# A chain of four image layers on one Trainium2 core: the step input multiplied on VectorE, and the last two pairs of sixteen states summed by TensorE

## The reference, cut to what matters

```
delta = softplus(einsum('blr,dr->bld', dt, W_dt) + b_dt)
A = -exp(A_log)
def step(hst, xs):
    d_t, B_t, C_t, u_t = xs
    dA = exp(d_t[:, :, None] * A)
    hst = hst * dA + (d_t * u_t)[:, :, None] * B_t[:, None, :]
    y_t = einsum('bdn,bn->bd', hst, C_t)
    return hst, y_t
y = ys + xc * Dp
y = y * silu(z)
```

## Time and profile before

| | |
|---|---|
| time, median of 3 runs | 5245.92 us (5242.39 to 5246.16) |
| the profiled execution's own time | 5247.66 us |
| its span | 5245.8 us |
| TensorE (PE) busy | 4574.1 us, 87% |
| VectorE (DVE) busy | 4798.9 us, 91% |
| ScalarE (ACT) busy | 3722.0 us, 71% |
| GpSimd (POOL) busy | 4717.1 us, 90% |
| mean granted TensorE clock | 0.971 |

### The profile page before, as it was taken

The page is one execution under the profiler, slowest core; times in us unless marked ns, Lnnn a source line. Parts: engine busy times, 40 slices in busy tenths (PEclk is TensorE's granted clock), DMA queues, the critical chain, the costliest instruction groups (busy, mean ns, idle before and its releaser), DMA issues.

```text
span 5245.8 us, 62166 instructions
## 1 busy us (share of the span) xinstructions
PE 4574.1 (87%) x17331; PEld 2625.0 (50%) x17331; DVE 4798.9 (91%) x5978; ACT 3722.0 (71%) x6077; POOL 4717.1 (90%) x3342
## 2 busy tenths in 40 slices
PE   7469999999999999999999999999999999999880
PEld 7125555555555555555555555555555555555450
DVE  4689999999999999999999999999999999999933
ACT  3457777777777777777777777777777777777642
POOL 0599999999999999999999999999999999999910
PEclk9679999999999999999999999999999999999995
DMA  4466666666666666666666666666666666666618
GB/s 142 154 237 234 232 243 244 238 236 242 241 232 238 245 241 236 234 249 238 226 241 250 236 236 234 250 238 227 241 248 236 235 241 243 240 230 244 235 73 324
DMA packets 199100, 1216.88 MB, mean 232 GB/s; under 512 B 27880, under 2 KB 28656, under 8 KB 67696
## 3 DMA queue, kind: packets, MB, share of 16 engines
q1 hardware_dynamic: 194416, 1196.26, 62.1%
q10 hardware_dynamic: 4352, 16.78, 0.8%
HBM read 1158.43 MB, written 54.53 MB: 231 GB/s over the span
## 4 chain that ended last, share of the span: by engine, by line
PE 57%; issue 12%; ACT 12%; DVE 12%; POOL 3%; DMA 2%; SPq 0%; DVEq 0%; ACTq 0%; POOLq 0%
PE psT L880 29%; PE psE L880 15%; PE psT L1058 6%; PE psY L880 6%; DVE hs L567 5%; DVE nm L587 3%; ACT da L752 3%; ACT pt L760 2%; ACT p L794 2%; DVE psD L554 2%; POOL pa L370 2%; ACT L722 1%; ACT xc L722 1%; PE psD L880 1%; POOL pa L376 1%
## 5 line engine op out<-in xcount | busy, mean ns | idle before, releaser
L370 POOL TENSOR_TENSOR pa<-hs,rows_all 128x1024 f32<-128x1024 f32 x1024 | 2416.4, 2360 | 8.0 <-DVE hs L567 3.4
L752 ACT ACTIVATE da<-delta,neg_a 128x512 f32<-128x512 f32 x2048 | 1410.0, 715 | 103.7 <-DVE hs L567 85.9
L376 POOL TENSOR_TENSOR pa<-pa 128x512 f32<-128x512 f32 x1024 | 1310.0, 1279 | 40.1
L554 DVE TENSOR_TENSOR psD<-rows_all,psU 128x512 f32<-128x512 f32 x2048 | 1303.0, 681 | 4.8 <-DMA rows_all<-bc_scratch 3.8
L567 DVE TENSOR_TENSOR_SCAN hs<-da,hlast,psD 128x512 f32<-128x512 f32 x1024 | 1266.6, 1263 | 4.0 <-ACT da L752 3.9
L567 DVE TENSOR_TENSOR_SCAN hs<-da,psD 128x512 f32<-128x512 f32 x1024 | 1204.1, 1202 | 2.2 <-POOL hlast L374 1.5
L880 PE MATMUL psT<-pt,va 128*128 128x256 f32 x4096 | 964.2, 381 | 0.0
L760 ACT ACTIVATE pt<-psT 128x512 f32<-128x512 f32 x1024 | 606.3, 592 | 334.9 <-PE psT L1058 332.4
L880 PEld LDWEIGHTS psT<-pt,va 128*128 128x128 f32 x4096 | 746.7, 190 | 161.6 <-issue 76.9
L1058 PEld LDWEIGHTS psT<-ident,p 128*128 128x128 f32 x4096 | 483.7, 141 | 519.0 <-issue 359.7
L794 ACT ACTIVATE p<-psE,nm 128x1024 f32<-128x1024 f32 x512 | 570.1, 1113 | 234.6 <-DVE nm L587 232.6
(11 more groups left out here) (180 smaller groups left out, 4841.7 us busy)
## 6 DMA issues: line engine op xcount, KB each, us to landing
rows_all<-bc_scratch SPq DMA_DIRECT2D x1024, 1024.0 KB, 4.7
xin<-x SPq DMA_DIRECT2D x40, 512.0 KB, 7.7
xres<-x SPq DMA_DIRECT2D x64, 256.0 KB, 6.1
x_scratch<-x SPq DMA_DIRECT2D x32, 512.0 KB, 5.5
f_scratch<-fa SPq DMA_DIRECT2D x32, 512.0 KB, 6.8
xres<-x SPq DMA_DIRECT2D x8, 512.0 KB, 3.7
x1g<-x SPq DMA_DIRECT2D x8, 512.0 KB, 3.6
fa<-x SPq DMA_DIRECT2D x8, 512.0 KB, 3.7
```

What stands on the lines that cost most here:

```text
L370: pool.tensor_tensor(pa[:, k % PROD, :, :], hs[:, sl, :, :], rows_all[:, slot, 2:4, :], ALU.mult).then_inc(S["prod"], 1)
L376: pool.tensor_tensor(pa[:, k % PROD, 0, :], pa[:, k % PROD, 0, :], pa[:, k % PROD, 1, :], ALU.add).then_inc(S["pair"], 1)
L554: dve.tensor_tensor(psD[:, j, :], rows_all[:, slot, j, :], psU[:, :], ALU.mult).then_inc(S["dbu_ok"], 1)
L752: act.activation(da[:, k % 2, j, :], delta[:, h, cols(ch)], ACT.Exp, scale=neg_a[:, h, 2 * q + j:2 * q + j + 1]).then_inc(S["da_ok"], 1)
```

## The change

Three things are changed.

1. `du` is no longer made on GpSimd. The multiplication L361 goes, and with it its waits. The copy on VectorE (`inputs`, L545) becomes a multiplication of delta and xc, both in SBUF, into `psU` in PSUM. The wait for the readers of `g` (`x1_mm`) moves from GpSimd to `gate` on VectorE.
2. In the round of the last two pairs of each half (k % 8 == 7, four times an image) GpSimd no longer makes the sum of four states (L380). TensorE adds the two pair sums by two matmuls with the identity instead of one. The semaphore that counts these matmuls is called `sum_mm`, and `summed(k)` gives its count after step k: five a half instead of four.
3. The four tables are written anew, with the same words but for the places.

```diff
@@ ORDER_PE
-            "energy7 add turna6 weigha2 turnb6",
-            "weighb2 resx turna7 residual",
-            "turnb7 weigha3 weighb3 query add",
+            "add turna6 energy7 weigha2 turnb6",
+            "weighb2",
+            "turna7 resx add residual turnb7 weigha3 weighb3 query",
             "",
-            "inner0 add inner1",
-            "key energy0",
+            "inner0 key inner1 add",
+            "energy0",
             "add",
-            "values energy1 turna0",
-            "gates1 turnb0 skip0 add energy2 gates0",
-            "rows turna1 turnb1",
-            "energy3 steps0 add",
-            "weigha0 steps1 weighb0 turna2 energy4 turnb2 turna3 skip1 turnb3",
-            "add",
-            "energy5 turna4 weigha1 turnb4 weighb1",
-            "turna5 energy6 turnb5 add",
+            "values energy1 turna0 skip0",
+            "turnb0 add gates1 gates0 energy2",
+            "turna1 rows turnb1",
+            "energy3 steps0 weigha0 add",
+            "steps1 weighb0 turna2 energy4 turnb2 skip1 turna3",
+            "add turnb3 weigha1 turna4 energy5",
+            "weighb1",
+            "turnb4 add turna5 turnb5 energy6",
@@ ORDER_DVE
             "dbu scan0 scan1 max6",
-            "dbu scan0 attend1 scan1 gate1",
+            "dbu scan0 attend1 scan1",
             "dbu max7 scan0 scan1",
-            "dbu recip3 attend2 scan0 normed scan1",
-            "dbu scan0 scan1 attend3",
+            "gate1 dbu scan0 attend2 scan1",
+            "recip3 dbu normed scan0 scan1 attend3",
             "dbu scan0 scan1",
             "dbu scan0 scan1",
             "dbu scan0 inputs scan1 max0",
             "dbu scan0 scan1 max1",
             "dbu scan0 scan1",
             "dbu scan0 max2 scan1",
-            "dbu gate0 scan0 scan1 max3",
-            "dbu recip0 scan0 recip1 scan1",
-            "dbu scan0 scan1 max4 attend0",
-            "dbu scan0 scan1 max5",
-            "dbu scan0 inputs recip2 scan1",
+            "dbu scan0 max3 gate0 scan1",
+            "dbu scan0 recip0 recip1 scan1",
+            "dbu scan0 attend0 scan1 max4",
+            "dbu scan0 scan1",
+            "dbu max5 scan0 inputs recip2 scan1",
@@ ORDER_ACT
...
-            "table decay0 copya1 exp2 decay1 rows",
-            "copyb1 decay0 decay1 sp0 exp3",
-            "decay0 sp1 decay1 copya2",
-            "decay0 ln0 copyb2 decay1 spread0 copya3 exp4",
-            "decay0 copyb3 ln1 decay1 copya4 exp5 copyb4",
+            "table copya1 exp2 decay0 decay1",
+            "rows copyb1 decay0 decay1 sp0 exp3",
+            "decay0 decay1 sp1",
+            "decay0 decay1 copya2 spread0 ln0 copyb2 ln1 copya3",
+            "exp4 copyb3 decay0 decay1 copya4 exp5 copyb4",
             "copya5 decay0 decay1 copyb5",
@@ ORDER_POOL
             "prod",
-            "prod delta0",
+            "delta0 prod",
+            "delta1 prod",
             "prod",
-            "prod delta1",
         ]
+
+        def summed(k):
+            return 5 * (k // PAIRS) + (k % PAIRS + 1) // 2 + k % PAIRS // (PAIRS - 1)
@@ step_size
-                    wait(pool, "delta_ok", fb, i)
-                    wait(pool, "xc_ok", fb, i)
-                    wait(pool, "x1_mm", fb - 1, fc + 1)
-                    pool.tensor_tensor(du[:, h, cols(fc)], delta[:, h, cols(fc)], xc[:, h, cols(fc)], ALU.mult
-                                       ).then_inc(S["du_ok"], 1)
@@ products
-                    wait(pool, "quad_mm", b, k // 2 - 1)
+                    wait(pool, "sum_mm", b, summed(2 * (k // 2) - 3))
...
-                    if k % 2:
+                    if k % 2 and k % PAIRS != PAIRS - 1:
@@ inputs
-                    wait(dve, "du_ok", b, k // PAIRS + 1)
+                    wait(dve, "delta_ok", b, k // PAIRS + 1)
+                    wait(dve, "xc_ok", b, k // PAIRS + 1)
                     wait(dve, "dbu_ok", b, 2 * k)
-                    dve.tensor_copy(psU[:, :], du[:, h, cols(ch)]).then_inc(S["u_ok"], 1)
+                    dve.tensor_tensor(psU[:, :], delta[:, h, cols(ch)], xc[:, h, cols(ch)], ALU.mult
+                                      ).then_inc(S["u_ok"], 1)
@@ gate
-                    wait(dve, "quad_mm", b, (NS * ch + PAIRS * (h + 1)) // 2)
+                    wait(dve, "sum_mm", b, summed(NS * ch + PAIRS * h + PAIRS - 1))
+                    wait(dve, "x1_mm", b - 1, ch + 1)
@@ sum_states
-                    wait(pe, "quad", b, (k + 1) // 2)
-                    mm(psY[:, :], ident[:, :], pa[:, k % PROD, 0, :], start=(q == 1), stop=(q == PAIRS - 1)
-                       ).then_inc(S["quad_mm"], 1)
+                    if q == PAIRS - 1:
+                        wait(pe, "pair", b, k + 1)
+                        for i in (k - 1, k):
+                            mm(psY[:, :], ident[:, :], pa[:, i % PROD, 0, :], start=False, stop=(i == k)
+                               ).then_inc(S["sum_mm"], 1)
+                    else:
+                        wait(pe, "quad", b, (k + 1) // 2 - k // PAIRS)
+                        mm(psY[:, :], ident[:, :], pa[:, k % PROD, 0, :], start=(q == 1), stop=False
+                           ).then_inc(S["sum_mm"], 1)
```

More of the change, by code:

```diff
@@ L178, in build @@
             dpre_mm=2 * NCH, sp_abs=2 * NCH, sp_relu=2 * NCH, sp_exp=2 * NCH, sp_ln=2 * NCH,
-            delta_ok=2 * NCH, du_ok=2 * NCH,
+            delta_ok=2 * NCH,
             u_ok=2 * NCH, dbu_ok=2 * STEPS, da_ok=2 * STEPS, h_ok=2 * STEPS,
-            hlast_ok=STEPS // 2, prod=STEPS, pair=STEPS, quad=STEPS // 2, quad_mm=STEPS // 2, g_ok=2 * NCH,
+            hlast_ok=STEPS // 2, prod=STEPS, pair=STEPS, quad=STEPS // 2 - NCH * NH, sum_mm=STEPS // 2 + NCH * NH, g_ok=2 * NCH,
             x1_mm=NCH, x1_ok=NCH, x1g_ok=NCH,
@@ L263, in build @@
             "dbu scan0 max2 scan1",
-            "dbu gate0 scan0 scan1 max3",
-            "dbu recip0 scan0 recip1 scan1",
-            "dbu scan0 scan1 max4 attend0",
-            "dbu scan0 scan1 max5",
-            "dbu scan0 inputs recip2 scan1",
+            "dbu scan0 max3 gate0 scan1",
[3 more added lines that the diff above has]
+            "dbu max5 scan0 inputs recip2 scan1",
         ]
         ORDER_ACT = [
[L272 to L275, removed]
+            "decay0 decay1 spread1 centre",
+            "exp6 rstd copya6 decay0 decay1",
+            "exp7 decay0 copyb6 spread2 copya7 decay1",
+            "residual copyb7 decay0 decay1",
+            "spread3 decay0 query decay1",
+            "xi0 decay0 decay1",
             "decay0 decay1",
-            "xi0 decay0 decay1 query",
-            "decay0 decay1",
-            "key decay0 decay1",
+            "decay0 key decay1",
             "decay0 xi1 decay1 exp0 value",
-            "decay0 copya0 exp1 decay1 copyb0 silu0 silu1 z1 z0",
-            "table decay0 copya1 exp2 decay1 rows",
-            "copyb1 decay0 decay1 sp0 exp3",
-            "decay0 sp1 decay1 copya2",
-            "decay0 ln0 copyb2 decay1 spread0 copya3 exp4",
-            "decay0 copyb3 ln1 decay1 copya4 exp5 copyb4",
+            "decay0 copya0 decay1 exp1 copyb0 silu0 silu1 z1 z0",
+            "table copya1 exp2 decay0 decay1",
[3 more added lines that the diff above has]
+            "exp4 copyb3 decay0 decay1 copya4 exp5 copyb4",
             "copya5 decay0 decay1 copyb5",
@@ L714, in front @@
                     if what == "xi":
-                        wait(act, "quad_mm", fb - 1, NS // 2 * (fc + 1))
+                        wait(act, "sum_mm", fb - 1, summed(NS * fc + NS - 1))
                         wait(act, "xi_mm", fb, 2 * fc + n + 1)
```

## The result

The changed kernel is slower: 5315.36 us (5314.09 to 5319.25), 1.0133 times the time before, with a 95% interval of 1.0121 to 1.0146. The profiled execution's span is 5312.3 us, 66.5 more than before. Measured from one first `dbu` to the next, image 0 takes 136.2 us instead of 143.8, image 1 160.1 instead of 151.7, and the 20 images of the new stage 152.7 each instead of 150.3. From image 0 to the start of image 31 that makes 67.2 us, the whole difference.

A forecast was written before the change was run, and what follows sets the result against it. GpSimd bounds the kernel, VectorE close behind; afterwards VectorE binds at 142.8 + 8.0 waits + 1.0 idle = 151.8 us an image. 31 images give +46.5, image 0 -9.5: 5283 us, +0.7%; range 5180 to 5364.

The forecast's parts named there:

- GpSimd is the bound; its list falls by 10.8 us to 139.5: GpSimd, per image: four L361 and four L380 go, each with its gap; 150.3 us of work becomes 139.5.
- A multiplication of two SBUF tensors waits for GpSimd: VectorE's new multiplication at L545: shared SBUF ports make it wait for GpSimd's instruction; group mean near 2.1 us.
- The six waits, 8.0 us: VectorE, per image: port waits of two multiplications each in rounds 7 and 15 and two `normed` in round 4.
- round 15 was taken at 1.2: VectorE's multiplication in round 15: port wait 0.1 to 0.7 or 2.0 to 2.3 us, taken as 1.2, twice an image.
- the walk: Round-by-round count of VectorE and GpSimd from the new tables, GpSimd starting only behind scan1; it gave the port waits.
- Round 7 was taken at 1.6: VectorE's multiplication in round 7: port wait at least 1.5 us behind GpSimd's L370 of round 6, twice an image.
- Idle time, 1.0 us: VectorE, per image: 3.8 us of waits shrink to 1.0 because attend0 and max4 no longer stand together; bounds 0 and 3.8.
- Image 0 gains 9.5 us, images 1 to 31 lose 1.5 each: Whole kernel: image 0, bound by GpSimd alone, -10.8 + 1.3; the other 31 go from 150.3 to 151.8 us.
- TensorE: 142.4 us, hidden by its waits: TensorE, per image: four added matmuls cost 4.2 us, making 142.4 of work, hidden in 12.0 us of idle time.
- The third rival: TensorE becomes the bound with its waits unchanged: 154.4 us an image, 5364 us; chance 0.12.
- The first rival: VectorE's port waits are short, 5.1 us an image, with no idle time: 147.9 us an image, 5162 us; chance 0.33.

The follow-up runs named there:

- M: Kernel before, old tables, with only VectorE's multiplication of delta and xc (part 1); GpSimd still sums all pairs: 5274.91 us, ratio 1.0064.
- S: Kernel before, old tables, with only TensorE summing the last two pairs (part 2); GpSimd keeps its multiplication: 5270.77 us, ratio 1.0047.
- T alone: Kernel before with the four new tables and no other edit: 5455.85 us, ratio 1.0404.
- `normed` first: Changed kernel with the multiplication directly behind dbu in rounds 7 and 15, and normed at the head of round 4: 5236.76 us, ratio 0.9986.

## Why the prediction was right

Forecast 5283 us, measured 5315; slower, and by the mechanism named: with the second operand in PSUM the kernel is faster than before (5138). Part of the closeness is luck. The waits were right in sum and not place by place (3), and the old tables give the same time (5319) with hardly any port wait, so the time alone would have proved nothing.

1. *GpSimd is the bound; its list falls by 10.8 us to 139.5.* Busy 139.5 us, and with the short gaps (2.2) 141.7, against 140.8 counted. It no longer binds in any kernel with M or S: it waits 5 to 13 us an image for scans there. The reading was too simple in one thing: S alone with the old tables, 5.5 us less on GpSimd, was slower. VectorE's longer waits for TensorE in that run speak for a second bound of nearly the same length, which the absence of GpSimd's own waits doesn't exclude.
2. *A multiplication of two SBUF tensors waits for GpSimd.* Mean 1.977 us, forecast 2.1; with a PSUM operand 0.673. In the 55 of the 80 cases that waited for a product the instruction ends 0.55 to 0.56 us behind GpSimd's; the other 25 took 0.67 us, because they started before GpSimd's next product or together with it. The rule of the Trainium skill (SBUF — State Buffer, "Who interferes with whom") that the prediction quotes agrees with both, and with the 0.673 us with one operand in PSUM.
3. *The six waits, 8.0 us.* Measured 4 x 1.30 + 2 x 1.16 = 7.5. By place: round 15 was taken at 1.2. It was 2.1 in the first chunk; in the second it was 2.1 in 15 images and nothing in 5, the two branches that the walk saw (it counted 2.3 for the longer one and cut it to 2.0; the longest wait was 2.2). Those five images last 151.2 us, the nine others with as much half clock 153.4: the wait is on the path at its full length. Round 7 was taken at 1.6, "at least 1.5", and was 1.5 in the second chunk but 0.0 in the first. There GpSimd's product of round 6 stood for TensorE's `add` (above), and VectorE came 0.06 us ahead of it; it took 2.82 us instead of 2.36. The walk let GpSimd start a round as soon as its scan was done and left this wait out. So the sum is right because two places at 1.2 were too short and one at 1.6 too long. VectorE's list is 150.5 us against 150.8, busy for 98.6% of the stage (over 99% was said).
4. *Idle time, 1.0 us.* This is the term that was too small: 2.2 us, 1.5 of them for scores. The reason given (max4 and attend0 apart) is borne out, no wait for `rb` is left; but VectorE's lateness comes back to it. At 2579.59 the multiplication waits, max0 ends at 2584.06, ScalarE's exponential follows, and TensorE waits for it. TensorE's timeline and windows of the changed kernel:

```profile
2585.36 2.87 PE L881 MATMUL psE<-ka,x 128*128 128x512 f32 x4 [2.25 <-ACT p L795]
2588.02 1.06 PE L1065 MATMUL psT<-ident,p 128*128 128x128 f32 x4
```

```profile
2583.10:2585.30 2.20, 0.01 (x1) 0.00 (x0) 2.20 (x4) 1.81 (x4) 2.20 (x1) 1.00 0.91 376
2585.30:2590.20 4.90, 4.84 (x11) 2.42 (x12) 4.26 (x5) 2.73 (x5) 3.77 (x4) 0.65 0.53 216
```

   After 2.25 us of standing the granted clock is at half for 3.4 us, the tile's scores take 2.87 instead of 1.88 us, and the next max waits. TensorE stands so in all 20 images (45.0 us, 20 times), the clock falls in 14 of them. With equal port waits the images with the stretch last 153.4 us and those without 152.9, so the clock itself is worth some 0.6 us in an image that has it. Of the 32 us between forecast and result the images behind image 1 have 23 (2.3 us each where 1.5 was said), image 1 has 7 and image 0 has 2.
5. *Image 0 gains 9.5 us, images 1 to 31 lose 1.5 each.* Image 0 gained 7.6. Image 1 was no steady image: it lost 8.5, with TensorE's clock at half for 25.6 us of it (before 15.2); what of the 8.5 is the clock's isn't shown. The others lost 2.3.
6. *TensorE: 142.4 us, hidden by its waits.* 142.6 us. Hidden under the new tables, where S even gains: 34 us beside M (5349 to 5315), 9 alone (5456 to 5447). Under the old tables it costs 44 us beside M (5275 to 5319) and 24 alone. The third rival, 154.4 us an image behind TensorE, comes near the old tables with both edits (153.1), not the changed kernel.
7. *The tables.* The prediction took them as given and counted only what they did to the waits of VectorE. Alone they cost 210 us, beside S 176 (5271 to 5447), beside M 74 (5275 to 5349), and beside both edits nothing (5319 with the old, 5315 with the new, within the noise). So in the changed kernel they take one loss away, VectorE's waits for TensorE, and bring another, the port waits of 1.3 us.

The first rival (short port waits, faster) was a real possibility: the old tables have waits of 0.2 us, and three lines of VectorE's order written otherwise give 5174 us. It didn't hold for these tables.

## What to carry to other kernels

Where VectorE and GpSimd are both as busy as here, moving an elementwise step with two SBUF operands from the one to the other doesn't free its time: price it at its length plus the rest of whatever GpSimd is doing then, look for the place in the order where GpSimd is waiting or in a short instruction, or give it one operand in PSUM. When three engines are within a few per cent of each other, shortening one need not show: 5.5 us less of 147 on GpSimd alone gave 0.5% more time. And an order is good or bad only with the lengths that it meets: the same tables cost 4% without the two edits and nothing with them. An in-order TensorE that stands two or three microseconds for a late operand pays for it twice if its granted clock then falls.

## What the runs showed of the hardware that was not expected

- VectorE wins the port against a GpSimd instruction that waits for the scan just ahead: `normed` directly behind scan1 took 0.67 us in all 40 cases, and GpSimd's product 2.73 us instead of 2.36.
- TensorE's granted clock fell to half behind waits of 1.45 + 3.21 us (6.8 us at half, twice an image, 40 of 40 times in T alone) and, in 14 of 20 images, behind one of 2.25 us (3.4 us at half). In the kernel before, whose longest single wait in the stage is 1.5 us, it stayed at full through all 20 images. But the longest single wait doesn't tell it: with `normed` first the clock fell in 8 of 20 images behind waits of 1.1 + 0.7 us, and without that step it never fell behind the same two waits; with both edits and the old tables it fell 13 times behind 1.45 us and a shorter wait.
- What 1.3 us less in one instruction is worth depends on what else waits there. The five images of the changed kernel that had no port wait in round 15 of the second chunk are 2.3 us shorter for 2.1 us of wait. 1.3 us taken from round 7 gave 1.2 us an image (5315 to 5277), by shorter waits for scores as much as by itself. 2 x 1.2 us taken from `normed` gave 0.7 us in the images at full clock and nothing in the mean (5236 and 5237).
